# Attention kernel on one core: heads change places in half of the queries, and steps are grouped by tile size

## What is computed

```python
def dilated_mask(seq_len):           # SEGMENT_LENGTH 64, DILATION_RATE 4
    local = seg[None, :] == seg[:, None]
    dil = (diff > 0) & (diff % DILATION_RATE == 0) & (diff <= DILATION_RATE * SEGMENT_LENGTH)
    return jnp.where(local | dil, 0.0, -jnp.inf)
q = (hidden_states @ w_q).reshape(B, S, H, Dh)      # H = 16 heads of Dh = 64; k and v alike
scores = jnp.einsum('bqhd,bkhd->bhqk', q, k) * scaling + mask[None, None]
attn = jax.nn.softmax(scores.astype(jnp.float32), axis=-1)
out = jnp.einsum('bhqk,bkhd->bqhd', attn, v).reshape(B, S, H * Dh)
return out @ w_o
```

## Time and profile before

| what | value |
|---|---|
| median of three executions | 473.95 us |
| profiled execution | 470.72 us, of which 468.8 us from the first to the last instruction |
| TensorE, VectorE, ScalarE, GpSimd busy | 95%, 85%, 71%, 63% |
| granted TensorE clock | 1.000 throughout |
| DMA | 40.53 MB, 135440 packets on SyncE's queue |

### The profile page before, as it was taken

How to read it: one execution, slowest core, us unless ns; L and a number is a source line. 1 busy time by engine, 2 the same in 40 slices (tenths; PEclk the granted TensorE clock), 3 DMA queues, 4 the chain that set the end, 5 groups by cost and what they waited for, 6 DMA issues and landing times.

```text
span 468.8 us, 17264 instructions
## 1 busy us (share of the span) xinstructions
PE 443.2 (95%) x6440; PEld 348.2 (74%) x6440; DVE 396.6 (85%) x1344; ACT 332.5 (71%) x975; POOL 296.1 (63%) x491
## 2 busy tenths in 40 slices
PE   6899989999999999999999999999876889999996
PEld 4677767888888888788788778888644658558675
DVE  5987859988898899889888698996899989999585
ACT  3487858877877777887786678677565579896523
POOL 4234638777666858676866587665777998655222
PEclk9999999999999999999999999999999999999999
DMA  6378692346435444344455555354000000000003
GB/s 224 127 206 232 169 293 52 73 94 131 88 74 111 78 79 97 78 90 84 109 118 125 121 123 105 60 119 96 1 1 0 0 2 1 1 0 2 1 0 91
DMA packets 136098, 40.53 MB, mean 86 GB/s; under 512 B 104976, under 2 KB 131024, under 8 KB 136016
## 3 DMA queue, kind: packets, MB, share of 16 engines
q1 hardware_dynamic: 135440, 38.38, 35.6%
q10 hardware_dynamic: 576, 1.05, 0.6%
HBM read 29.44 MB, written 9.96 MB: 84 GB/s over the span
## 4 chain that ended last, share of the span: by engine, by line
PE 64%; DVE 11%; DMA 7%; SPq 6%; POOL 5%; ACT 4%; issue 3%; ACTq 0%; DVEq 0%; POOLq 0%
PE psum L423 11%; PE psum L465 9%; PE psum L1187 5%; PE psum L485 5%; PE psum L499 4%; PE psum L1182 4%; PE psum L511 4%; PE psum L404 4%; PE psum L496 4%; DMA w_rows_dram<-st 3%; PE psum L406 3%; PE psum L405 3%; DMA st<-w_rows_dram 2%; SPq L292 2%; DMA arena<-in_L_attn_w_q_dram 2%
## 5 line engine op out<-in xcount | busy, mean ns | idle before, releaser
L949 POOL TENSOR_SCALAR pband<-pband,fac 128x192 f32<-128x192 f32 x256 | 104.6, 429 | 83.8 <-DVE fac L772 83.6
L570 ACT ACTIVATE pband<-pband,st 128x192 f32<-128x192 f32 x256 | 113.2, 448 | 0.1
L720 DVE CUSTOM_DVE_ANT_0 pband<-psum,band_mask 128x192 f32<-128x192 f32 x256 | 76.1, 353 | 1.0 <-PE psum L423 0.9
L423 PE MATMUL psum<-keys,q_class 64*64 64x192 f32 (+2 forms) x1536 | 66.2, 275 | 0.0
L465 PEld LDWEIGHTS psum<-ident,pband 128*128 128x128 f32 x384 | 45.2, 141 | 22.4 <-issue 13.0
L423 PEld LDWEIGHTS psum<-keys,q_class 64*64 64x64 f32 x1536 | 57.4, 133 | 2.9 <-issue 2.0
L465 PE MATMUL psum<-ident,pband 128*128 128x128 f32 x384 | 53.1, 274 | 3.4 <-DVE pt L781 3.2
L570 ACT ACTIVATION_READ_ACCUMULATOR pband<-pband,st 128x1 f32 x256 | 49.5, 193 | 0.0
L931 POOL COPY keys<-k_rows 128x512 f32<-128x512 f32 x32 | 36.2, 1132 | 17.5 <-issue 9.0
L781 DVE COPY pt<-psum 128x512 f32<-128x512 f32 x64 | 43.7, 682 | 1.4 <-PE psum L465 0.8
L939 POOL COPY q_class<-q_rows 128x512 f32<-128x512 f32 x32 | 36.3, 1135 | 11.0 <-ACT q_rows L610 11.0
(11 more groups left out here) (212 smaller groups left out, 1088.4 us busy)
## 6 DMA issues: line engine op xcount, KB each, us to landing
v_rows_dram<-arena SPq DMA_DIRECT2D x32, 256.0 KB, 3.1
v_both<-v_rows_dram SPq DMA_DIRECT2D x32, 256.0 KB, 3.8
v_seg<-v_rows_dram SPq DMA_DIRECT2D x64, 128.0 KB, 3.6
v_side<-v_rows_dram SPq DMA_DIRECT2D x96, 64.0 KB, 2.6
w_rows_dram<-st SPq DMA_DIRECT2D x64, 8.0 KB
st<-w_rows_dram SPq DMA_DIRECT2D x64, 8.0 KB
arena<-_attn_hidden_states_dram SPq DMA_DIRECT2D x4, 256.0 KB, 4.3
out_dram<-x SPq DMA_DIRECT2D x4, 256.0 KB, 2.3
```

What stands on the lines that cost most here:

```text
L423: return pe.matmul(bank[2 * r + head][rows, at:at + y.shape[1]], x, y, start=True, stop=True, skip_group_check=True)
L570: act.activation(x, x, ACT.Exp, bias=mine[:, head:head + 1], scale=-1.0, accum_out=mine[:, 2 + head:3 + head]).then_inc(s_exp, 1)
L720: dve.tensor_tensor_reduce(pband[:, G % P_SLOTS, c, head, :], bank[2 * r + head][:, at:at + BAND], band_mask[:, (0, 1, 1, 2)[w], SEG * (1 ...
L949: pool.tensor_scalar(x, x, fac[:, F % 2, 1, c, head:head + 1], 1.0, ALU.mult, ALU.mult).then_inc(s_scaled, 1)
```

## The change

- `place`: in the second half of every 128 queries (partitions 64 to 127 of the scores) the two heads change places, in the score banks and in everything that follows. So sides and segments of the second half use the two tiles off the diagonal, `v_side` is loaded so, and `v_seg` holds both heads on both halves of the partitions (two DMAs of 256 KB a set instead of 128 KB).
- The weighed values of the two halves go to banks 6 and 7 (`half_bank`). Each `v_both` product of 128 queries becomes two of 64. `take_out` reads both banks in one instruction; `output` writes to bank 6 (`mixed_bank`), so `weigh` waits for `accumulate` of the set before (`s_acc`).
- From step 6 on the projections go to banks 0 and 1, once `band_max` and `seg_max` of part 0 of set `t - 3` have read them; scores wait until keys and queries are copied out.
- `scores` is split in `band_scores` and `segment_scores` (both parts each); the second waits for the first (`s_band`).
- In the loop each engine's list is laid out anew; maxima, exponentials, differences and factors are of sets one step older, and the loop has one step more (`DRAIN`). Prologue and drain, with the four later layers, have new orders too (not shown).

```diff
-    turn_bank, out_bank, shared_bank = bank[4:6], bank[6], bank[7]
+    turn_bank, half_bank = bank[4:6], bank[6:8]
+    mixed_bank, spare_bank = half_bank
...
+    def row_bank(x, name):
+        return half_bank[1] if x < FIRST_STEP else bank[("query", "key").index(name)]
+    def wait_rows(pe, x, name):
+        if x >= FIRST_STEP:
+            pe.wait_ge(s_max, 8 * (x - 3) + 4)
+            pe.wait_ge(s_seg, 2 * (x - 3) + 1)
+            return
...
+    def place(head, half):
+        return head ^ half
...
+                wait_rows(pe, t, name)
+                to, cols = row_bank(t, name), slice(w * WT, (w + 1) * WT)
...
+            def band_scores(G):
...
+                for r in range(2):
+                    wait(pe, s_max, 8 * (G - 1) + 4 * (r + 1))
+                    wait(pe, s_seg, 2 * (G - 1) + r + 1)
+                    if r == 0 and FIRST_STEP <= G + 2 < NS_ALL:
+                        pe.wait_ge(s_query, G + 3)
+                        pe.wait_ge(s_key, G + 3)
+                    for c in (2 * r, 2 * r + 1):
+                        at = BAND * (c % 2)
+                        x0, x1 = (q_class[DH * head:DH * (head + 1), G % ROW_SLOTS, c, :] for head in range(2))
+                        y0, y1 = (keys[DH * head:DH * (head + 1), p % 2, c, P * w:P * w + P + 2 * SEG] for head in range(2))
+                        product(1, 1, at, x1, y1[:, SEG:SEG + BAND])
+                        product(1, 0, at, x1, y1[:, 0:BAND])
+                        product(0, 0, at, x0, y0[:, SEG:BAND])
+                        product(0, 1, at + SEG, x0, y0[:, SEG:BAND])
+                        product(0, 0, at + P, x0, y0[:, 0:SEG])
+                        last = product(0, 1, at, x0, y0[:, BAND:BAND + SEG])
+                    last.then_inc(s_band, 1)
...
+            def segment_scores(G):
...
+                for r in range(2):
+                    pe.wait_ge(s_band, 2 * G + r + 1)
+                    for a in (2 * r, 2 * r + 1):
+                        at = SEG_AT + SEG * (a % 2)
+                        for head in range(2):
+                            dims = slice(DH * head, DH * (head + 1))
+                            for half, rows in enumerate(halves):
+                                cols = slice(P * a + SEG * half, P * a + SEG * (half + 1))
+                                last = pe.matmul(bank[2 * r + place(head, r)][rows, at:at + SEG],
+                                                 q_rows[dims, G % ROW_SLOTS, cols], k_rows[dims, G % ROW_SLOTS, cols],
+                                                 start=True, stop=True, skip_group_check=True)
+                    last.then_inc(s_score, 1)
...
-                    wait(pe, s_out, U)
+                    wait(pe, s_acc, U)
...
-                    if b < 2:
-                        c, head = 2 * b + k // 2, k % 2
+                    c, at = 2 * b + k // 2, k % 2
+                    for half in range(2):
+                        head = place(at, half)
                         dims = slice(DH * head, DH * (head + 1))
-                        last = pe.matmul(by_class[dims, c, :], v_both[:, c, w, dims], turned[:, P * k:P * (k + 1)],
+                        last = pe.matmul(by_class(half)[dims, c, :], v_both[:, c, w, dims],
+                                         turned[:, P * k + SEG * half:P * k + SEG * (half + 1)],
                                          start=(b == 0 and k < 2), stop=False, skip_group_check=True)
...
+            def weigh_sides(U):
...
+                for k in range(4):
+                    for half, side in enumerate((2 * w - 2, 2 * w + 1)):
+                        if not 0 <= side < 2 * (NW - 1):
                             continue
                         for head in range(2):
+                            dims, at = slice(DH * head, DH * (head + 1)), place(head, half)
+                            rows = slice(DH * at, DH * (at + 1))
+                            last = pe.matmul(by_class(half)[dims, k, :], v_side[rows, k, side, :],
+                                             turned[rows, P * k + SEG * half:P * k + SEG * (half + 1)],
+                                             start=False, stop=False, skip_group_check=True)
+                last.then_inc(s_pv[0], 1)
...
+            def weigh_segments(U):
...
+                for a in range(TW // 2):
+                    for s in range(2):
+                        for half in range(2):
+                            k = TW // 2 * half + a
+                            for head in range(2):
+                                dims, at = slice(DH * head, DH * (head + 1)), place(head, half)
+                                rows = slice(DH * at, DH * (at + 1))
+                                last = pe.matmul(half_bank[half][dims, P * a + SEG * s:P * a + SEG * (s + 1)],
+                                                 v_seg[rows, 2 * (TW * w + k) + s, dims],
+                                                 turned[rows, P * k + SEG * s:P * k + SEG * (s + 1)], start=False,
+                                                 stop=(a == 1 and s == 1), skip_group_check=True)
+                last.then_inc(s_pv[1], 1)
...
             for t in range(FIRST_STEP, DRAIN):
+                turn(t - 6, 0)
+                turn(t - 6, 1)
                 project(t, 1)
+                output(t - 7)
+                project(t, 0)
+                turn(t - 6, 3)
+                turn(t - 6, 2)
                 weigh(t - 6, 0)
                 weigh(t - 6, 1)
-                turn(t - 6, 3)
-                output(t - 7)
-                turn(t - 5, 0)
-                weigh(t - 6, 2)
-                scores(t - 2, 0)
-                weigh(t - 6, 3)
-                scores(t - 2, 1)
-                project(t, 0)
-                turn(t - 5, 1)
-                turn(t - 5, 2)
+                band_scores(t - 2)
+                segment_scores(t - 2)
+                weigh_sides(t - 6)
+                weigh_segments(t - 6)
...
-                exp_difference(t - 4)
-                take_out(t - 6)
+                odd_turned(t - 6, 1)
+                exp_difference(t - 5)
                 take_queries(t)
-                odd_turned(t - 5, 1)
-                take_keys(t + 1)
-                band_exps(t - 2, 0)
-                odd_turned(t - 5, 3)
-                seg_exps(t - 2)
-                band_exps(t - 2, 1)
+                take_keys(t)
+                seg_exps(t - 3)
+                odd_turned(t - 6, 3)
+                band_exps(t - 3, 0)
+                band_exps(t - 3, 1)
...
+                take_out(t - 6)
...
-                differences(t - 4)
-                even_turned(t - 5, 0)
...
+                seg_max(t - 3, 0)
+                band_max(t - 3, 0)
+                seg_max(t - 3, 1)
+                even_turned(t - 6, 0)
+                differences(t - 5)
...
-                factors(t - 4)
-                band_max(t - 2, 0)
-                seg_max(t - 2, 0)
-                even_turned(t - 5, 2)
-                seg_max(t - 2, 1)
-                band_max(t - 2, 1)
-                seg_sums(t - 2)
-                accumulate(t - 6)
+                accumulate(t - 7)
+                factors(t - 5)
+                band_max(t - 3, 1)
+                seg_sums(t - 3)
+                even_turned(t - 6, 2)
...
+                scale_band(t - 5, 0)
                 scale_band(t - 5, 1)
+                scale_seg(t - 5)
+                queries_by_class(t)
                 keys_by_class(t)
-                scale_seg(t - 5)
-                scale_band(t - 4, 0)
-                queries_by_class(t - 1)
```

More of the change, by code:

```diff
@@ L159, in attention @@
         v_side = sb("v_side", [P, DIL, 2 * (NW - 1), DH])
[L160 removed]
+        v_seg = sb("v_seg", [P, T // SEG, P])
         o_sb = sb("o_sb", [P, WT])
@@ L436, in scores @@
-                for a in (2 * r, 2 * r + 1):
-                    at = SEG_AT + SEG * (a % 2)
-                    for head in range(2):
-                        dims = slice(DH * head, DH * (head + 1))
-                        for half, rows in enumerate((first, second)):
-                            cols = slice(P * a + SEG * half, P * a + SEG * (half + 1))
-                            last = product(head, rows, at, q_rows[dims, G % ROW_SLOTS, cols],
-                                           k_rows[dims, G % ROW_SLOTS, cols])
@@ L444, in scores, with product @@
-                last.then_inc(s_score, 1)
+                pe.wait_ge(s_qclass, G + 1)
+                pe.wait_ge(s_kclass, min(G + 2, NS_ALL) if w < NW - 1 else G + 1)
+                def product(head, half, at, x, y):
+                    rows = halves[half]
+                    return pe.matmul(bank[2 * r + place(head, half)][rows, at:at + y.shape[1]], x[:, rows], y, start=True,
+                                     stop=True, skip_group_check=True)
+                for r in range(2):
[15 more added lines that the diff above has]
+                    last.then_inc(s_band, 1)
@@ L488, in weigh @@
```

(17 more changed lines are left out.)

285 lines of the change are left out of this document (126 added, 159 removed), and 24 rows, old and new, of the table STEPS.

## The result

| | before | changed kernel |
|---|---|---|
| median of four executions each | 473.89 us | 481.06 us |
| ratio to before, 95% interval | | 1.0156, 1.0106 to 1.0206 |
| profiled execution, span | 470.72, 468.8 us | 479.68, 477.8 us |
| first loop step's output to the 25th (24 steps) | 218.2 us | 223.0 us |
| from there to the end of set 30's step | 52.5 us | 58.3 us |

A forecast was written before the change was run, and what follows sets the result against it. TensorE's list was taken to bound the kernel up to 342 us. Gains of 16.4 (loop), 4.2 (290 to 342) and 1.3 (ahead of 71) make 21.9 us: 448.8 against 470.72 profiled, 452 on the median; range 444 to 468 with rivals.

The forecast's parts named there:

- Step 8.43 forecast as 8.35: One loop step on TensorE: 4.25 + 1.09 + 3.0 = 8.35 us in both kinds, where the mean was 9.03.
- `v_both` 1.09 as 1.09: 32 passes of 64 columns, pairs at 0.058 us like `v_seg`: 0.93 + 0.16 = 1.09 us; upper end 0.81 more a step.
- sides at 14 ns: Side passes on four tiles start 14.6 ns apart instead of 29.2, strided outputs included, with w = 1 or 2.
- no wait for maxima over 0.3 us: `project(t, 1)` now waits for part 0's maxima on VectorE: 0 to 0.3 us, taken as 0.
- the two rules of the Trainium skill: Non-contiguous access slows matmuls significantly; about 60 cycles a matmul up to 64 columns, so nothing under 25 ns.
- Rivals 1 to 3: Sides stay at 29 ns, +7.5 us, 0.06; four tiles not parallel, 22 us, 0.08; `v_both` pairs keep 0.109, 26 us, 0.06.
- rival 5: ScalarE's ring, forecast at 8.0 us, lengthens through waits on VectorE and holds up `output`: 9.5 costs +13 us; chance 0.07.
- Ahead of the loop: Before 71 us: first loop step 0.45, one change of size less for each of four scores 0.8, together 1.3 us gained.
- The step that failed: Values of both heads double the `v_seg` transfers; the 16 DMA engines are 0.47 busy, so cost nothing.
- Rival 4: Exchange or start-up waits grow as steps shorten and `v_seg` shares the queue: +6 us, 458; chance 0.13.
- 16.4: Gain of the 24 loop steps, 71 to 290 us: 12 x 0.92 + 12 x 0.45 = 16.4 us.
- The drain: Seven sets weighed from 290 to 342 us: TensorE saves 4.7 us, 4.2 taken, since 1.5 of waits stand there.

The follow-up runs named there:

- run 7: The changed kernel with values loaded for the first pair of heads alone and used for all pairs: 461.1 us, ratio 0.972.
- run 2: The changed kernel with `v_seg` loaded as before the change (half its bytes; result not whole): 472.1 us, ratio 0.987.
- run 1: The changed kernel with 128 more waits, long met, ahead of all of TensorE's work: 491.5 us, ratio 1.030.
- run 13: The changed kernel with `v_seg` in four DMAs of 64 KB, two behind the fetch of statistics, VectorE's list unchanged: 496.2 us, ratio 1.044.

## Why the prediction was wrong

**TensorE's terms held for a step that nothing disturbs.** Step 8.43 forecast as 8.35; `v_both` 1.09 as 1.09; sides at 14 ns; steps of one length for all w (run 7); no wait for maxima over 0.3 us. The trace again disagrees with the two rules of the Trainium skill that the prediction weighed ("PSUM — Partial Sum Buffer", Specifications, and "TensorE: Matmul & The Clock Gate", Back-to-back issue gap): strided outputs go at 14 ns a pass, as unstrided scores do, which is under 25. Rivals 1 to 3 are out by the rows of the step. So is rival 5: `output` never waited for ScalarE in the loop for over 0.2 us. Ahead of the loop 1.7 us were gained (69.19 against 70.91; 1.3 forecast), behind it nothing, as forecast.

**The step that failed** is the one on `v_seg`: "the 16 DMA engines are 0.47 busy, nothing, though the exchange shares them". The values loaded for a set rose from 704 to 960 KB on average (`v_both` 256, `v_side` 192, `v_seg` 256 or 512), the share to 0.61, and this costs 1.6% with the old passes and 2.9% with the new. Rival 4 named the queue but only the exchange as its victim, and at 6 us, where the loop alone was 21 us over its forecast (222.99 against 218.17 - 16.4 = 201.8). The victim that the prediction did not have at all was TensorE's own code. The added bytes are 13 us of the 29 between 452 and 481. With the traffic of before the changed kernel (run 2, 0.987 of 473.9) is still 16 us above the forecast; in its one trace 10.3 us of the loop are late blocks, a cost for which the sum had no term at any traffic. Even without loads the loop misses 201.8 by 7.3 us, and only 2.4 of these are idle times of over 0.15 us. The loop's account: 24 steps of 8.43 make 202.3; gaps at block ends 14.3; one wait for `accumulate` 1.2, one for maxima 0.3; the rest, 4.9, is put down to the clock's fall at 123.5 (below) and the overlap of neighbouring passes that each gap breaks, up to 0.2 each (this split is worked out, not measured apart).

**Why the changed kernel suffers more.** This is read from the traces' block ends, not tested by itself, and it covers a third of the gaps' length. With the short passes of a step in one run, some blocks are used up fast: without loads, 10 of the 39 blocks that lie from 71 to 290 us last 3.1 to 3.6 us, in the kernel before 2 of 33 (3.3 each). Under the changed kernel's traffic the transfer of the next block starts, in most blocks, 0.8 to 2.0 us behind the first instruction of the running one (0.2 to 1.0 in most short blocks without loads), takes 0.9 to 1.7, and at the gaps 1.2 to 1.6 more pass before use. Seven of the 16 gaps, 4.6 us in all, end such a fast block, which then lasts 3.7 to 4.4 us, gap included. The other nine, 9.7 us with the three longest among them, end blocks of 5.3 to 7.8 us whose successor's transfer started only 2.8 to 5.4 us in; in the kernel before the latest such start is 3.5 us in, without loads 4.0. Five of the nine blocks stand right behind a fast one, the three with the longest gaps do not. Why those transfers start so late stays open, and with it most of why these lists suffer more than the old ones.

**The drain** was to give 4.2 us and cost 5.8. Gaps "issue" are 1.4 of it, `accumulate` and the weights' transposes waiting for VectorE 3.1, GpSimd 0.9, the clock some 1.7. Without loads it takes 53.3, against 50.8 for the kernel before without loads: here TensorE's savings are worth nothing even so. That others' results set the pace there is argued from these waits, not tested. The term was sized from one row of busy time.

## What to carry to other kernels

On an engine that issues short instructions back to back, its own code is a DMA stream: count instructions per microsecond as bytes, and look where blocks end, before making passes shorter. Do not cost added transfers at nothing because the engines' mean share is low; ask who else waits in that queue, the engine's code and small exchanges first. An idle time "issue" in the middle of a list without waits is to be counted in instructions from the last one.

## What the runs showed of the hardware

- TensorE's code comes in blocks of 16 KB, 256 instructions; in the changed kernel's trace every block took 0.9 to 1.7 us and was used no sooner than 1.2 us behind its landing (in run 1 one took 3.2). The Trainium skill, "Runtime: NRT & Kernel Launch", Instruction fetch mechanics, gives the same size and says that crossing a block's end is mostly hidden; the first agrees with the 56 packets here. The second agrees with the kernel before, which has no such idle time in its loop, and not with the changed kernel, with 14.3 us at 16 block ends of 24 steps.
- An idle time of 2.27 us in the loop was enough to bring the granted clock to its lower level, 1.2 GHz, for 3.4 us:

```profile
117.00:123.50 6.50, 4.59 (x162) 4.22 (x160) 5.68 (x26) 5.52 (x20) 5.64 (x11) 1.00 0.72 153
123.50:127.00 3.50, 3.14 (x32) 2.92 (x32) 1.04 (x4) 0.87 (x2) 0.66 (x1) 0.51 0.42 83
```

  It did not fall behind the gap of 2.56 us that ended at 261.66; in run 13 it fell behind gaps of 2.31 and 2.95 us in the loop. Where it falls, a gap costs more than its length: the step with the gap of 2.27 took 12.19 us, where 8.43 and 2.27 make 10.70.
- Four tiles take one 64x64 pass in 14 ns, two tiles one in 29, on strided outputs as on plain ones; 64-column passes of 128 rows go in pairs at 60 ns.
